# Two attentions of a transformer kernel: narrow score units as one matmul over heads and queries

## What is computed

```
scores = jnp.einsum('bhqd,bhkd->bhqk', q, k) * scale
probs = jax.nn.softmax(scores + causal, axis=-1)
out = jnp.einsum('bhqk,bhkd->bhqd', probs, v)
```

## Time and profile before

| what | value |
|---|---|
| median of three runs | 1535.99 us (1528.93 to 1537.26) |
| profiled execution, first to last instruction (the time taken for it) | span 1535.8 us |
| mean granted TensorE clock | 0.909 |
| TensorE matmul busy | 1313.7 us, 86% |
| TensorE weight load busy | 774.5 us, 50% |
| VectorE busy | 976.1 us, 64% |
| ScalarE busy | 692.4 us, 45% |
| GpSimd busy | 115.2 us, 7% |

### The profile page before, as it was taken

One profiled execution on the slowest core, in us unless ns is written; L12 is line 12 of the kernel. 1 busy time (PEld: TensorE's weight loads), 2 busy tenths in 40 slices (PEclk: granted clock), 3 DMA queues, 4 the chain that ended last, 5 costly groups with the idle time before them and its releaser, 6 DMA issues. The chain is left out here.

```text
span 1535.8 us, 21410 instructions
## 1 busy us (share of the span) xinstructions
PE 1313.7 (86%) x7772; PEld 774.5 (50%) x7772; DVE 976.1 (64%) x1750; ACT 692.4 (45%) x1319; POOL 115.2 (7%) x155
## 2 busy tenths in 40 slices
PE   4688999999999999966999996526898888789998
PEld 3344444454545454444888874413343333256886
DVE  4455464545555454146999985756777666257998
ACT  2232334342424252433666665421566556525664
POOL 0000000000000000000000000120211111020000
PEclk9698999999999999987999998855899989868998
DMA  3101111120201020104576640022222210102220
GB/s 103 40 15 34 29 34 34 33 48 15 48 19 43 15 43 15 30 0 96 130 159 146 150 92 1 1 35 90 56 55 57 47 47 20 43 21 78 76 103 28
DMA packets 51476, 81.61 MB, mean 53 GB/s; under 512 B 16749, under 2 KB 34453, under 8 KB 47445
## 3 DMA queue, kind: packets, MB, share of 16 engines
q1 hardware_dynamic: 51004, 79.40, 21.1%
q10 hardware_dynamic: 384, 1.05, 0.6%
HBM read 63.75 MB, written 5.68 MB: 45 GB/s over the span
## 5 line engine op out<-in xcount | busy, mean ns | idle before, releaser
L621 DVE TENSOR_REDUCE mraw<-ps 128x1 f32<-128x512 f32 (+3 forms) x304 | 192.7, 659 | 131.1 <-PE ps L507 74.0
L1329 PE MATMUL ps<-qA 128*128 128x512 f32 x960 | 252.9, 400 | 15.2 <-POOL qA L1439 10.6
L723 ACT ACTIVATE shared<-ps 128x512 f32<-128x512 f32 (+1 forms) x216 | 119.4, 567 | 263.3 <-PE ps L540 261.9
L1046 DVE TENSOR_REDUCE mraw<-ps 128x2 f32<-128x1024 f32 (+3 forms) x160 | 173.7, 1114 | 67.6 <-PE ps L954 46.1
L1329 PEld LDWEIGHTS ps<-qA 128*128 128x128 f32 x960 | 182.1, 192 | 64.2 <-POOL qA L1439 12.3
L1101 ACT ACTIVATE shared<-ps 128x512 f32<-128x512 f32 (+2 forms) x320 | 154.4, 561 | 124.7 <-PE ps L970 124.4
L539 PE MATMUL ps<-qA,kH 128*128 128x512 f32 (+3 forms) x384 | 167.8, 447 | 5.8 <-DMA qB<-mT 5.8
L501 PE MATMUL ps<-kH,qA 128*128 128x512 f32 (+3 forms) x384 | 138.8, 415 | 34.9 <-DVE qA L611 18.8
L1393 ACT CAST qA<-shared 128x512 fp32r<-128x512 f32 x160 | 99.3, 621 | 90.4 <-DVE shared L1531 88.9
L1341 PE MATMUL ps<-qA,kH 128*128 128x512 f32 x480 | 136.3, 393 | 4.1 <-DVE qA L1455 4.1
L540 PE MATMUL ps<-qB,kL 65*128 65x512 f32 (+3 forms) x384 | 132.8, 356 | 0.0
(11 more groups left out here) (247 smaller groups left out, 1747.1 us busy)
## 6 DMA issues: line engine op xcount, KB each, us to landing
shared<-comb SPq DMA_DIRECT2D x92, 256.0 KB, 4.3
qB<-qA SPq DMA_DIRECT2D x16, 512.0 KB, 4.8
rB<-a0rec_dram SPq DMA_DIRECT2D x60, 128.0 KB, 2.9
shared<-comb SPq DMA_DIRECT2D x7, 1024.0 KB, 4.4
rB<-a1rec_dram SPq DMA_DIRECT2D x28, 128.0 KB, 2.6
e0wUp<-in_w SPq DMA_DIRECT2D x48, 64.0 KB, 4.6
qA<-q_split SPq DMA_DIRECT2D x24, 128.0 KB
q_split<-qA SPq DMA_DIRECT2D x4, 512.0 KB
```

Source lines behind the costliest of these rows:

```text
L621: nc.vector.tensor_reduce(out[:, h0:h0 + n_h, qt % 4], src, AX, ALU.max).then_inc(w_free, 1)
L723: nc.scalar.activation(probs(n)[:, hs[0]:hs[-1] + 1, lo:512], src, ACT.Exp, scale=scale)\
L1046: nc.vector.tensor_reduce(out[:, :, js[0]:js[-1] + 1, qt % 4], src, AX, ALU.max).then_inc(x_free, 1)
L1329: ins = nc.tensor.matmul(bank[0:M, :], w[par][:, at:at + M], h[:, cols], start=(r == 0), stop=(r == 2))
```

## The change

In both attentions the loop over the heads of a job is gone. The job's heads are a slice of the middle dimension of the query tensor, so the moving operand is heads by queries, and the output is the bank's first `len(hs) * w` columns seen as heads by queries. In `qA`, `qB` and `Q` a head's row has `S` = 1024 floats, so from one head's piece to the next the address moves by 4096 bytes. In the second attention the heads 0 and 2 (or 1 and 3) are neighbours, since `Q` is stored for each row tile by `h // 2`. Jobs of one head (widths 512 and 384) are written in the same form with one head.

```
-                    for at, h in enumerate(hs):
-                        out = score_bank(s)[:, at * w:(at + 1) * w]
-                        nc.tensor.matmul(out, k.kH[par][:, keys], k.qA[par][:, h, cols], start=True, stop=False)
-                        ins = nc.tensor.matmul(out, k.kL[par][0:hd + 1, keys], k.qB[par][0:hd + 1, h, cols],
-                                               start=False, stop=True)
-                    ins.then_inc(s_full, 1)
+                    heads = slice(hs[0], hs[-1] + 1)
+                    out = score_bank(s)[:, 0:len(hs) * w].rearrange("p (h q) -> p h q", q=w)
+                    nc.tensor.matmul(out, k.kH[par][:, keys], k.qA[par][:, heads, cols], start=True, stop=False)
+                    nc.tensor.matmul(out, k.kL[par][0:hd + 1, keys], k.qB[par][0:hd + 1, heads, cols],
+                                     start=False, stop=True).then_inc(s_full, 1)
...
-                    for slot, h in enumerate(hs):
-                        ins = nc.tensor.matmul(score_bank(s)[:, slot * w:(slot + 1) * w],
-                                               kOne[g % 3][rows, kt * P:(kt + 1) * P],
-                                               Q[g % 3][rows, h // 2, qc * 512 + lo:(qc + 1) * 512],
-                                               start=True, stop=True)
-                    ins.then_inc(s_full, 1)
+                    pair = slice(hs[0] // 2, hs[-1] // 2 + 1)
+                    out = score_bank(s)[:, 0:len(hs) * w].rearrange("p (h q) -> p h q", q=w)
+                    nc.tensor.matmul(out, kOne[g % 3][rows, kt * P:(kt + 1) * P],
+                                     Q[g % 3][rows, pair, qc * 512 + lo:(qc + 1) * 512],
+                                     start=True, stop=True).then_inc(s_full, 1)
```

## The result

Over six runs each, the changed kernel takes 1524.16 us (1519.82 to 1526.81) against 1536.18 us before (1528.93 to 1538.35). The ratio of the two is 0.9928, with a 95% interval of 0.9901 to 0.9955, so the gain is 7 to 15 us and the medians say 12. The forecast was 1528.8 us, a gain of 7.2. The direction was right and 1524.16 us lies within the stated range, but the gain is nearly 5 us larger than the sum.

A forecast was written before the change was run, and what follows sets the result against it. TensorE was taken to lead the first attention, with the second shared more evenly; 6.1 + 0.6 + 0.5 = 7.2 us off the 1535.8 us span gives 1528.6, 1528.8 as median; own range 1524 to 1533, overall 1522 to 1537.

The forecast's parts named there:

- The step lengths: First attention: four-head jobs fall from 0.95 to 0.57 us (6.1 us in all), two-head from 0.59 to 0.57 (0.6 us).
- The named signs: 224 fewer matmuls and weight loads, first attention ending about 6.7 us earlier, stages between and after the attentions unchanged in length.
- Does the gain reach the end?: First attention: work behind four-head jobs moves earlier as a whole, full 6.7 us taken; a DMA wait might cost 2.4 us.
- Rival A: DMA round trips of sums, row maxima and second query copy absorb the gain: 1536 us if all, 1532 half; chance 0.2.
- The size of the work term: First attention: 16 four-head jobs at 0.38 us and 32 two-head jobs at 0.02 us, 6.7 us saved.
- The second attention: 16 units of 128 columns on two row tiles gain 0 to 1.1 us, 0.5 taken; 256-wide units gain nothing.
- The new shape: Moving operand jumps 4 KB after each head; taken to cost nothing, at the far end 0.11 us a jump.
- Rival C: Every jump between heads restarts the stream, 160 jumps at 0.11 us in the first attention: 1546 us; chance 0.08.
- Rival B: Weight loads not hidden, so each of 160 + 64 removed matmuls gives back 0.11 us, 24.6 us: 1511 us; chance 0.04.
- the long stall at 336.11: First attention: TensorE waits 1.92 us for VectorE's split of line 611, in a chain said to move as a whole.
- The period "of about 74.3 us": First attention's loop time per group of heads, expected to fall from 74.3 to about 73.5 us.

The follow-up runs named there:

- four_as_pairs: The changed kernel with each four-head job of the first attention as two pairs of heads, four matmuls of 256 columns instead of two of 512: 1526.43 us, ratio to before 0.9930.
- the filled kernels: Kernel before and changed kernel, each with seven bf16 matmuls put into long TensorE stalls of the first attention: 1528.17 us before; changed 1521.31 and 1518.27 us.
- a8_only: The kernel before with matmuls merged in the second attention alone: 1538.56 us, ratio to before 1.0010.
- two_only: The kernel before with only the two-head jobs (256 queries a head) of the first attention merged: 1536.14 us, ratio to before 0.9992.
- after_padded: The changed kernel with the first matmul of each four-head job issued three times: 1543.65 us, ratio to before 1.0031.

## Why the prediction was right, and where it was short

The mechanism of the sum is right and gives 7.4 of the 12 us. That the time fell within the forecast's own range of 1524 to 1533 us, by 0.2 us, is luck in part: the range held 4 us for differences between runs, and they covered a gain through the clock that the sum did not have.

- **The step lengths** held. The four-head job went from 0.95 to 0.58 us (0.57 said), the two-head job saved next to nothing, and the 160 + 64 removed weight loads brought nothing beyond the pace of the 128-column pieces. The reason given, 128 columns paced by their own weight load, fits `four_as_pairs` and the steps at 324.02 us. The named signs held too: 224 matmuls and loads fewer, and from the last score matmul of the first attention to the first of the second 388.8 us, against 388.7. One did not: the last score matmul of the first attention starts at 644.4 us against 658.1, 13.7 us earlier in place of about 6.7.
- **"Does the gain reach the end?"** Yes. Everything behind a four-head job moved as a whole. The DMA wait of the sums took nothing: VectorE waits 23.0 us for it in the first attention, 23.3 before, and TensorE's score matmuls wait 5.8 us for a DMA in both. Rival A is refuted.
- **The size of the work term** was a little low. The sum had 6.7 us for the first attention, the filled kernels show 7.4: by the periods without a low stretch a four-head job gives 0.40 us in place of 0.38, and a two-head job about 0.025 in place of 0.02.
- **The second attention**: 0.5 us was taken, `a8_only` shows no gain (0.9984 to 1.0037), though 0.5 us is too small for that interval to exclude. The pair itself is 0.22 us, so the 0.06 us a unit exist in the steps; whether waits take them or the noise hides them is not shown.
- **The new shape** costs nothing. Rival C is refuted by the changed kernel's own rows.
- **Rival B** (weight loads not hidden, 24.6 us) is refuted by the result (the interval ends at 15 us), by the rows of `four_as_pairs` and by `two_only` (64 loads at 0.11 us would be 7 us, the interval ends at 4). The trace does not agree with the rule of the Trainium skill, page "TensorE: Matmul & The Clock Gate", section "Part 3: Packing small matmuls — row/col tiling", that a weight load overlaps with running matmuls only when the row groups differ: these matmuls use the same rows, and their loads are hidden at 256 and 512 columns (steps of 0.12 and 0.24 us).
- **The term that was missing** is one for the clock. The sum took the granted clock as given, by "0.98 to 1.00" in the earlier trace rows, and priced the long stall at 336.11 as a wait alone. That one stall is indeed followed by no low stretch, but the same stall of five other groups is. The period "of about 74.3 us" was not the loop's own. It is 73.3 us, plus 1.0 to 1.5 us in every group in which the clock falls after the stall. The prediction also expected the period to fall to 73.5 us. Groups of the changed kernel with a low stretch do show 73.3 to 74.0, groups without one 72.4. The clock is worth 4 to 5 of the 12 us: 12 less 7.4 by the medians, 3.8 by the profiles.

**Open.** Why the merged kernels have fewer low stretches is not settled, and neither is how much of the difference in the start-up would come again. The stall is as long as before (1.92 us in both), it is followed by a low stretch in some groups only, and in the later groups `after_padded`, with dense matmuls and the old length, has as many as before. That speaks for where in time the stalls fall, not for how dense the jobs are, but one kernel is thin evidence. The next step would be the unchanged kernel with idle time added or removed elsewhere in the group.

## What to carry to other kernels

Merging matmuls that share their weights pays where each streams its columns in less time than the distance between weight loads, here at 128 columns of fp32r and not at 256: compare the distances between starts at each width before counting instructions. A stall of TensorE near 2 us can cost twice, as here, once as a wait and again when the clock falls behind it, so periods of a loop should be compared group by group, and only those at one clock. A few matmuls into a bank that is free anyway kept the clock up through such stalls here.

## What was not expected of the hardware

- A stall of TensorE of only 1.9 us in an otherwise busy stream was followed by 3.4 us at 1.2 GHz in five places of the first attention of the kernel before; each cost 1.0 to 1.5 us. Seven bf16 matmuls in the stall, 1.7 us in all, removed every one of them, in three profiles of two kernels.
- Two executions of the same code differed by 10 us of low clock in the start-up of the loop, and by 5.5 us in the length of the first attention. The whole spans were 2.7 us apart.
- A moving operand of four pieces of 128 columns, 4 KB apart, streams as fast as 512 adjacent ones (0.24 us at line 540).
